# Gate and up of the last six token tiles as one Strassen product, and the convolution moved to the down phase

## What is computed

```python
x = x + 0.5 * ffn(layernorm(x))
x = x + s4(layernorm(x))
x = x + 0.5 * ffn(layernorm(x))

def qlinear(x, q, scale, A, Bm):          # q: int32 levels 0 to 15
    w = (q - 7.5) * (scale * 0.005)[:, None]
    return x @ w.T + 0.02 * (x @ A @ Bm)  # rank 32

ffn(x) = qlinear(silu(qlinear(x, gate...)) * qlinear(x, up...), down...)   # 512 -> 1376 -> 512
s4(u)  = causal convolution of u with a kernel K of length 512, along the features, + D * u
```

## Time and profile before

| | us |
|---|---|
| median of three runs | 608.82 |
| range of the three | 608.34 to 610.92 |
| the profiled execution's own time | 609.25 |
| its span (first to last instruction) | 607.5 |

### The profile page before, as it was taken

How to read it: one execution, slowest core, us unless ns; L and a number is a source line. 1 busy time by engine, 2 the same in 40 slices (tenths; PEclk the granted TensorE clock), 3 DMA queues, 4 the chain that set the end, 5 groups by cost and what they waited for, 6 DMA issues and landing times.

```text
span 607.5 us, 9590 instructions
## 1 busy us (share of the span) xinstructions
PE 584.9 (96%) x3630; PEld 341.3 (56%) x3630; DVE 339.2 (56%) x693; ACT 282.4 (46%) x625; POOL 85.3 (14%) x97
## 2 busy tenths in 40 slices
PE   2799999999999999999999999999999999999997
PEld 2444674457644666445764457644575545754475
DVE  6487575774579727358563584335833467433334
ACT  3676324662277512657226662266623555136631
POOL 4337701100012000023001130012100010000000
PEclk9999999999999999999999999999999999999999
DMA  8994400003002500001301023000322002240001
GB/s 290 397 296 169 70 14 5 1 12 65 13 18 36 81 11 16 18 18 35 75 14 19 17 52 62 10 18 18 68 46 79 1 1 50 29 148 1 0 1 71
DMA packets 67630, 35.63 MB, mean 59 GB/s; under 512 B 56160, under 2 KB 60448, under 8 KB 67584
## 3 DMA queue, kind: packets, MB, share of 16 engines
q1 hardware_dynamic: 66768, 34.87, 22.4%
q10 hardware_dynamic: 816, 0.14, 0.1%
HBM read 17.43 MB, written 4.19 MB: 36 GB/s over the span
## 4 chain that ended last, share of the span: by engine, by line
PE 89%; DVE 5%; ACT 3%; issue 1%; DMA 1%; DVEq 0%; ACTq 0%
PE bank L1062 46%; PE down_acc L1022 27%; PE bank L1078 6%; PE down_acc L1172 4%; PE bank L988 2%; PE bank L1039 2%; PE bank L1155 1%; ACT p_stack L495 1%; DVE z L656 1%; DMA X<-in_x 1%; DVE z L658 1%; DVE zs L649 1%; DVE hT L678 0%; ACT bank L533 0%; ACT PdT L522 0%
## 5 line engine op out<-in xcount | busy, mean ns | idle before, releaser
L1022 PE MATMUL down_acc<-dw,hT 128*128 128x256 f16 (+3 forms) x1408 | 184.4, 286 | 0.0
L533 ACT ACTIVATE bank<-bank,scales 128x512 f32<-128x512 f32 (+1 forms) x176 | 115.8, 659 | 125.7 <-PE bank L1062 125.0
L1062 PE MATMUL bank<-xT,gw 128*128 128x512 f16 (+1 forms) x696 | 164.5, 379 | 2.3 <-ACT work L545 2.1
L1062 PE MATMUL bank<-xT,uw 128*128 128x512 f16 (+1 forms) x696 | 164.5, 379 | 0.2 <-DVE work L722 0.2
L1022 PEld LDWEIGHTS down_acc<-dw,hT 128*128 128x128 f16 (+1 forms) x1408 | 136.0, 98 | 38.5 <-issue 0.6
L722 DVE TENSOR_TENSOR work<-work,bank 128x512 f32<-128x512 f32 (+1 forms) x88 | 60.4, 687 | 138.3 <-PE bank L1078 128.7
L1062 PEld LDWEIGHTS bank<-xT,uw 128*128 128x128 f16 (+1 forms) x696 | 69.6, 100 | 81.1 <-DVE work L722 0.8
L1062 PEld LDWEIGHTS bank<-xT,gw 128*128 128x128 f16 (+1 forms) x696 | 68.4, 100 | 78.7 <-ACT work L545 4.6
L678 DVE SCALAR_TENSOR_TENSOR hT<-work,hT 128x512 f16<-128x512 f32 (+1 forms) x88 | 67.1, 763 | 19.6 <-ACT hT L538 19.5
L538 ACT ACTIVATE hT<-work 128x512 f16<-128x512 f32 (+1 forms) x88 | 55.4, 630 | 31.5 <-DVE work L722 31.5
L545 ACT ACTIVATE work<-bank 128x512 f32<-128x512 f32 (+1 forms) x88 | 51.8, 588 | 10.5 <-PE bank L1078 10.5
(11 more groups left out here) (145 smaller groups left out, 386.5 us busy)
## 6 DMA issues: line engine op xcount, KB each, us to landing
out_x<-X SPq DMA_DIRECT2D x16, 256.0 KB, 2.6
X<-in_x SPq DMA_DIRECT2D x1, 2048.0 KB, 14.8
gq_raw<-in_tables SPq DMA_DIRECT2D x1, 2048.0 KB, 10.5
gq_raw<-in_gate_q_t SPq DMA_DIRECT2D x2, 768.0 KB, 11.6
uq_raw<-in_up_q_t SPq DMA_DIRECT2D x2, 768.0 KB, 11.6
dq_raw<-in_down_q_t SPq DMA_DIRECT2D x1, 1536.0 KB, 14.1
work<-in_b SPq DMA_DIRECT2D x2, 688.0 KB, 9.2
X<-in_x SPq DMA_DIRECT2D x4, 256.0 KB, 5.5
```

The source lines that it names most:

```text
L533: return nc.scalar.activation(acc, acc, ACT.Copy, scale=scales[0:rows[m], g, m:m + 1])
L1022: last = mm(down_acc[b][:, c, 0:width], hT[0:rows[m], m, a, j * P:(j + 1) * P], dw[0:rows[m], m, c, 0:width], start=(m == 0 and a == 0), s ...
L1062: last = mm(dst[0:r, :], w[:, c, cols], xT[:, a, c, :], start=(c == 0 and a == 0), stop=(c == KH - 1 and a == 1))
```

## The change

Tiles 0 and 1 (of eight, counted from 0; `n < FAST`) keep the plain products. In tiles 2 to 7 gate and up of a block are one 2 x 2 product by Strassen's method in Winograd's form. The left factor has the four quarters UP1, UP2, GATE1, GATE2 (up or gate weights, first or second half of K), the right one z's quarters B11, B12, B21, B22 (half of K, half of the 512 tokens). Seven products of 128 rows, K = 256 and 256 tokens (each four matmuls of 256 columns: two chunks, high and low) replace eight.

- The weight sums S1 to S4 are formed once on GpSimd (`weight_sums`, four instructions of 128 x 2752, exact in fp16). z's sums T1 to T4 are formed in f32 on VectorE for each tile (`z_apply`, `z_differences`, `z_sums`), rounded on ScalarE (`z_high`), the rest formed on GpSimd (`z_low`). B12 itself is not kept: `p_product` uses T1 + B11 for it.
- P1, P1+P6 and P1+P6+P7 grow in one bank. ScalarE copies each state, scaled, to SBUF (`t_up`, `t_gate`), and VectorE adds the copies, scaling what stands in the PSUM banks (`up_scaled`, `gate_scaled`), ahead of the low-rank matmuls (now two of 256 columns each for gate and for up).
- h's split into high and low moves from ScalarE and VectorE to GpSimd (`h_split`) in blocks 0 to 9 of the fast tiles.
- The convolution's products and additions move to the down phase of tiles 2 to 5. The state-space part on VectorE moves from tiles 1 and 2 to tile 0's down phase and tile 1, the load of the tables behind the resolvents.
- The down banks are now shared with the blocks' banks; `pd_transpose` and `down_low` share one bank in fast tiles. z's transposes are four per tile, each of 128 tokens x 1792 columns (before: 1024). Many buffers share memory.

The core of the diff:

```diff
-Z_SCALE = 2.0 ** 11
+Z_SCALE = 2.0 ** 9
...
+    FAST = 2
...
+    CONV_IN = 2
...
+    T3, B22, B11, B21, T1, T4, T2 = range(7)
+    UP1, UP2, GATE1, GATE2, S1, S2, S3, S4 = range(0, 16, 2)
...
+            def weight_sums():
+                pool.wait_ge(s_gcast, len(CHUNKS))
+                pool.wait_ge(s_ucast, len(CHUNKS))
+                for i, (o, a, b, op) in enumerate(((S1, GATE1, GATE2, ALU.add), (S3, UP1, GATE1, ALU.subtract),
+                                                   (S2, S1, UP1, ALU.subtract), (S4, UP2, S2, ALU.subtract))):
+                    if i >= 2:
+                        pool.wait_ge(s_wsum, (1, 3)[i - 2])
+                    pool.tensor_tensor(w[:, o:o + 2, :], w[:, a:a + 2, :], w[:, b:b + 2, :], op).then_inc(s_wsum, 1)
...
+            def h_split(n, m):
+                b, r = m % 2, rows[m]
+                pool.wait_ge(f.h[b], uses(n, m) + 1)
+                pool.tensor_scalar(hT[0:r, m, 0, :], h32[0:r, b, :], 1.0, 0.0, ALU.mult, ALU.add)\
+                    .then_inc(f.hhi[b], 1)
+                pool.wait_ge(f.hhi[b], uses(n, m) + 1)
+                pool.tensor_tensor(hT[0:r, m, 1, :], h32[0:r, b, :], hT[0:r, m, 0, :], ALU.subtract)\
+                    .then_inc(f.hlo[b], 1)
...
+            def z_low(n, j, half):
+                q, ops = 2 * (n - FAST) + j, (slice(0, 4), slice(4, 7))[half]
+                pool.wait_ge(f.zq_hi, 4 * q + 3 + half)
+                pool.tensor_tensor(z16[:, j, 1, ops, :], zs[:, ops, :], z16[:, j, 0, ops, :], ALU.subtract)\
+                    .then_inc(f.zq_lo, 1)
...
+            weight_sums()
...
+            for n in range(FAST, N2):
+                more, c = n + 1 < N2, conv_group(n)
+                if c is not None:
                     conv_rstds(c)
-                    conv_low(c * TS)
-                tile_rstds(n + 1, range(0, 2))
-                if convs:
-                    conv_low(c * TS + 1)
-                tile_rstds(n + 1, range(2, TS))
-                if convs:
+                if more:
+                    ln_rstd(n + 1, 0, 1)
+                for m in range(M - 1):
+                    h_split(n, m)
+                    if more and m == 3:
+                        z_low(n + 1, 0, 0)
+                        ln_rstd(n + 1, 2)
+                    if more and m == 4:
+                        z_low(n + 1, 0, 1)
+                    if more and m == 5:
+                        ln_rstd(n + 1, 3)
+                    if c is not None and m in (6, 8):
+                        conv_low(c * TS + (m - 6) // 2)
+                if c is not None:
                     conv_low(c * TS + 2)
...
+            def fast_blocks(n, c):
+                for m in range(M):
+                    s, r, k = m % 2, rows[m], block(n, m)
+                    sums = bank[4 * s + 3][0:r, 0:HH]
+                    act.wait_ge(f.p1, k + 1)
+                    after(act, f.up_s, k - 1)
+                    if m == 1:
+                        act.wait_ge(f.x_out, n * TS)
+                    nc.scalar.activation(t_up[s][0:r, 0, :], sums, ACT.Copy, scale=scales[0:r, 1, m:m + 1])\
+                        .then_inc(f.t11, 1)
+                    act.wait_ge(f.p5, k + 1)
+                    after(act, f.gate_s, k - 1)
+                    nc.scalar.activation(t_gate[s][0:r, 1, :], bank[4 * s + 1][0:r, 0:HH], ACT.Copy,
+                                         scale=scales[0:r, 0, m:m + 1]).then_inc(f.t5, 1)
+                    act.wait_ge(f.p6, k + 1)
+                    nc.scalar.activation(t_up[s][0:r, 1, :], sums, ACT.Copy, scale=scales[0:r, 1, m:m + 1])\
+                        .then_inc(f.t12, 1)
+                    if m:
+                        sum_silu(n, m - 1)
+                    if n + 1 < N2 and 2 <= m <= 5:
+                        z_high(n + 1, 0, m - 2)
+                    if c is not None and m in (1, 7, 9):
+                        conv_norm(c * TS + (1, 7, 9).index(m))
+                    if c is not None and m in (6, 8, 10):
+                        conv_high(c * TS + (m - 6) // 2)
+                    act.wait_ge(f.p7, k + 1)
+                    nc.scalar.activation(t_gate[s][0:r, 0, :], sums, ACT.Copy, scale=scales[0:r, 0, m:m + 1])\
+                        .then_inc(f.t21, 1)
...
+            def z_differences(n, j):
+                q = 2 * (n - FAST) + j
+                dve.wait_ge(f.zs, n * TS + 2 * j + 2)
+                V.tensor_tensor(zs[:, T1:T1 + 2, :], zs[:, 0:2, :], zs[:, B11:B21 + 1, :], ALU.subtract)\
+                    .then_inc(f.z_d, 1)
+                dve.wait_ge(f.z_d, q + 1)
+                V.tensor_tensor(zs[:, T4, :], zs[:, T1, :], zs[:, T4, :], ALU.subtract).then_inc(f.z_t, 1)
+            def z_sums(n, j):
+                q = 2 * (n - FAST) + j
+                dve.wait_ge(f.z_t, 2 * q + 1)
+                V.tensor_tensor(zs[:, T2, :], zs[:, B22, :], zs[:, T1, :], ALU.subtract)
+                V.tensor_tensor(zs[:, T3, :], zs[:, B22, :], zs[:, T3, :], ALU.subtract).then_inc(f.z_t, 1)
...
+            def z_step(n, m):
+                if m == 0:
+                    ln_stats(n, 0, 1)
+                elif m == 4:
+                    ln_stats(n, 2)
+                elif m == 6:
+                    ln_stats(n, 3)
+                elif m in (1, 8):
+                    z_apply(n, m // 8)
+                elif m in (2, 9):
+                    z_differences(n, m // 9)
+                elif m in (3, 10):
+                    z_sums(n, m // 10)
...
+            def up_scaled(n, m):
+                s, r, k = m % 2, rows[m], block(n, m)
+                dve.wait_ge(f.p3, k + 1)
+                dve.wait_ge(f.t12, k + 1)
+                V.scalar_tensor_tensor(up_sums(m), up_sums(m), scales[0:r, 1, m:m + 1], t_up[s][0:r, :, :],
+                                       ALU.mult, ALU.add).then_inc(f.up_s, 1)
+            def gate_scaled(n, m):
+                s, r, k = m % 2, rows[m], block(n, m)
+                dve.wait_ge(f.t21, k + 1)
+                V.scalar_tensor_tensor(gate_sums(m), gate_sums(m), scales[0:r, 0, m:m + 1], t_gate[s][0:r, :, :],
+                                       ALU.mult, ALU.add).then_inc(f.gate_s, 1)
...
+            def fast_blocks(n):
+                for m in range(M + 1):
+                    if m:
+                        up_scaled(n, m - 1)
+                        gate_scaled(n, m - 1)
+                    if n + 1 < N2:
+                        z_step(n + 1, m)
+                    if m:
+                        dve.wait_ge(f.lr_up, block(n, m - 1) + 1)
+                        h_product(n, m - 1, up_sums(m - 1))
...
+                    ops = ((B11, 0), (B21, 2)) if s < 2 else ((T1, 0), (B11, 0), (B22, 2))
+                    terms = [(xT[:, a, 2 * op + k, j * P:(j + 1) * P], c + k)
+                             for op, c in ops for k in range(2) for a in range(2)]
...
+                if n >= FAST:
+                    after(pe, f.dsum, n * TS + j)
...
+            def part(m, dst, blocks, op, first, ks=(0, 1)):
+                r, cols = rows[m], slice(m * P, m * P + rows[m])
+                for k in ks:
+                    for a in range(2):
+                        last = mm(dst[0:r, 0:HH], w[:, blocks + k, cols], xT[:, a, 2 * op + k, :],
+                                  start=(first and k == 0 and a == 0), stop=(k == 1 and a == 1),
+                                  skip_group_check=True)
+                return last
...
+            def fast_blocks(n):
+                c = conv_group(n - 1)
+                for m in range(M):
+                    s, k = m % 2, block(n, m)
+                    up_1, up_2, gate_1, gate_2 = bank[4 * s:4 * s + 4]
+                    if m == 0:
+                        for j in range(2):
+                            pe.wait_ge(f.xTq[j], 32 * (n - FAST + 1))
+                        pe.wait_ge(f.p_stack, (n + 1) * TS)
+                        if n == FAST:
+                            pe.wait_ge(s_wsum, 4)
+                            pe.wait_ge(s_kscale, 1)
+                            pe.wait_ge(f.dsum, n * TS)
+                        if c is not None:
+                            pe.wait_ge(c_out, (c + 1) * TS)
+                    if m == 1:
+                        for b in range(2):
+                            pe.wait_ge(f.d_read[b], 2 * n)
+                    pe.wait_ge(f.silu[s], uses(n, m))
+                    part(m, gate_2, UP1, B11, True).then_inc(f.p1, 1)
+                    part(m, gate_1, GATE2, T4, True)
+                    pe.wait_ge(f.h[s], uses(n, m))
+                    part(m, up_2, S1, T1, True).then_inc(f.p5, 1)
+                    pe.wait_ge(f.t11, k + 1)
+                    part(m, gate_2, S2, T2, False).then_inc(f.p6, 1)
+                    if m == 0:
+                        pe.wait_ge(f.dsum, n * TS)
+                    part(m, up_1, UP2, B21, True, (0,))
+                    if m:
+                        low_rank(n, 0, m - 1)
+                    part(m, up_1, UP2, B21, False, (1,))
```

(69 more changed lines are left out.)

805 lines of the change are left out of this document (436 added, 369 removed).

## The result

The changed kernel takes 611.93 us (median of 20 runs, 610.89 to 617.23), the kernel before 609.42 (20 runs, 608.34 to 610.92). The ratio of the means is 1.0067 [1.0044, 1.0091]: 0.7% slower (0.4% by the medians), where the forecast was 600.0 with a range of 588 to 614. The profiled execution took 616.48 us (span 614.4); it is one of nine of the 20 that stand at 616.5 to 617.2, the other eleven stand at 610.9 to 612.0.

A forecast was written before the change was run, and what follows sets the result against it. The prediction took TensorE's nearly gapless stream of columns as the bound. Its terms, -25.1 + 2.7 + 2.1 + 1.2 + 2.4 + 4.0 + 4.0 = -8.7 us, took the profiled 609.25 to 600.5, adjusted to the median 600; range 588 to 614.

The forecast's parts named there:

- Weight sums: Tile 0's down phase: VectorE's last h split and an X addition wait for GpSimd's sums, +4 us, bounds 0 and 10.
- Gate and up: Blocks of six tiles: fewer matmul columns on TensorE, a tile's 42.7 us become 38.5, -25.1 us in all.
- Start of a tile: Block 1 of tiles 3 and 4: low-rank product waits 1.2 us for VectorE's scaled sums, +2.4 us.
- End of a tile: Before the last down transpose: TensorE waits about 0.35 us for ScalarE's P split and PdT copy, six times, +2.1 us.
- Tile 2's start: Tile 2's first product waits for tile 1's last dsum behind the Toeplitz split on VectorE, +1.2 us, between 0 and 3.5.
- The lock within a block: Fast blocks: z's differences at block 9 wait for GpSimd, 0.8 us late, five tiles, +4.0 us, bounds 0 and 15.
- ScalarE's copies: Within a fast block: 256-column copies out of PSUM taken at 0.40 us each, between 0.15 and 0.66, and covered.
- +2.7: Low-rank P: two of four P products have 12 matmuls in place of 8, 0.45 us a tile, six times.
- (3): Rival: GpSimd paces the fast blocks, five tiles each lose about 3.5 us, 618 us; chance 0.20.
- (2): Rival: VectorE or ScalarE paces the blocks, 3.85 us instead of 3.50, 606 to 612 us; chance 0.15.

The follow-up runs named there:

- e1: Changed kernel without the four weight sums, original weight blocks in place of S1 to S4 (wrong results in tiles 2 to 7): 600.11 us.
- e7: Changed kernel with the third weight sum also waiting for the second, so two stand back to back: 612.14 us.
- e2: Changed kernel with each weight sum on GpSimd waiting for the one before: 608.28 us.
- e3: Changed kernel with the weight sums on VectorE, two behind the last h split of tile 0 and two behind that of tile 1: 599.50 us.
- e9: As e3, fast tiles' h split back on ScalarE and VectorE, the high half behind the same block's last copy: 613.78 us.
- e5: As e3, fast tiles' h split back on ScalarE and VectorE, the high half behind the next block's silu: 676.45 us.
- e4: Changed kernel with the sums on GpSimd cut into 32 pieces of 344 columns, each waiting for the one before: 603.53 us.
- e6: As e8, and tile 0's first reciprocals moved behind P's split in its down phase: 593.70 us.
- e8: As e3, in fast tiles one of two statistics moved from block 0 to 1 and first-half z steps one block later: 595.14 us.

## Why the prediction was wrong

The failed step is **"Weight sums"**, "+4, bounds 0 and 10". The instruction was sized well (forecast 5.9 us, measured 5.46), and the forecast named two kinds of victim, the last h split and the X additions. It failed in assuming that each "can wait for the rest of a 5.9 us instruction". The split of block 9, which it didn't count, waited for three sums, since they stood back to back (TensorE waited 9.23 us for it), and the last one for the fourth (5.07): 14.3 us of waiting for h, where it had "some 2 us". The low clock adds more, as the P products above show. In tile 0's down phase the sums cost 16.6 us (44.6 against e1's 28.0), and 11.8 by the medians of the whole: above the bound of 10 either way. The X additions weren't hit at all, as the stall had carried them past the sums' end.

The Trainium skill (SBUF — State Buffer, Who interferes with whom) says that a VectorE instruction with two SBUF inputs contends with a GpSimd one that reads SBUF, calls the shared port pair an exclusive lock, and has issue order decide who blocks. The rows agree on which instructions are hit (17.00 us for L893, 0.68 for L887). By that rule alone the wait is one instruction's length, which is what I took; the 17.00, 11.67 and 6.33 us of the changed kernel, e7 and e2 show that a waiting VectorE isn't let in between two that stand back to back. Nor did the order of issue help: in the changed kernel the split stands at 69.80 and the first sum at 70.19.

The rest of the sum, step by step:

- **Gate and up**, -25.1 (3.50 us a block): right. The low-rank products of tile 2 come at 199.03 and 202.52, 3.49 apart, in slots of 0.109 (two start-to-start slots of low-rank products are 0.22):

```profile
199.03 0.38 PE L1315 MATMUL banks<-PT,gb_w 128*128 128x256 f16 x2 [0.17 <-DVE banks L908]
...
202.52 0.38 PE L1315 MATMUL banks<-PT,gb_w 128*128 128x256 f16 x2
```

- **Start of a tile**, stall 1.2 in tiles 3 and 4: right in place and cause. Tile 3's stands at 1.64 us, the sum is 4.1 in five waits, against +2.4. The forecast put the low-rank product 50 slots into the tile, but block 0 has no low-rank products, so it is 46, or 5.0 us; with that its own sum gives 6.7 - 5.0 = 1.7:

```profile
272.16 0.38 PE L1315 MATMUL banks<-PT,gb_w 128*128 128x256 f16 x2 [1.64 <-DVE banks L908]
```

- **End of a tile**, 0.35 us each: wrong, it costs nothing. The wait is there with 0.22 us, but the kernel before has one of the same length in each tile, ahead of its third `down_low`, and there it is gone: 1.6 us in seven waits in both profiles. The first row is of the kernel before, the second of the changed one:

```profile
306.78 0.39 PE L1039 MATMUL bank<-db_w,PdT 128*128 128x512 f16 x1 [0.22 <-ACT PdT L522]
...
338.23 0.39 PE L1292 MATMUL banks<-db_w,PdT 128*128 128x512 f16 x1 [0.22 <-ACT PdT L622]
```

- **Tile 2's start**: 1.3 against +1.2. TensorE's wait for the Toeplitz matrix's maximum grew from 0.3 to 1.1 us, which the sum doesn't have.
- **The lock within a block**, +4.0: too dear. The differences of z did take 1.26 us, as forecast, and ahead of them the two scalings of z, which I hadn't named, took 2.29 in place of 0.99. But only one low-rank product between them is late: one block of 3.82 us and the next of 3.56 in each of tiles 2 to 5, 0.4 a tile, some 1.5 in all:

```profile
223.02 2.29 DVE L833 TENSOR_SCALAR zs<-X,meanvar,rstd 128x512 f32<-128x512 f32 x2
...
227.16 1.26 DVE L840 TENSOR_TENSOR zs<-zs 128x512 f32<-128x512 f32 x1
```

- **ScalarE's copies** of 256 columns took 0.474 us against 0.40, and stayed covered.
- **Not in the sum**: the state-space vectors (2.0 us) and reciprocals (1.73) ahead of P's split in tile 0's down phase. The prediction costed no move of them; it took 1.75 us. Nor does it have the 2.0 us ahead of the down phase.

From tile 1's start on, the terms -25.1 + 2.7 + 2.1 + 1.2 + 2.4 + 4.0 = -12.7 stand against the measured -13.6. That they come so close is partly luck: +2.1 that didn't come and +4.0 that was 1.5 stand against starts too small by 1.7. With the sizes found, and 66 blocks shorter by 3.88 - 3.495, it is -25.4 + 2.7 + 0 + 1.3 + 0.8 + 4.1 + 1.5 = -15.0, and the 1.4 between them stays open. Tiles 3 and 4 each take 73.13 us in place of 74.61 where the terms give -1.4. In e3, without the sums on GpSimd, the whole kernel takes 599.5. The forecast without its +4 is 596, so its 600 and this 599.5 agree by luck too; but most of the gain that I saw in the change is there once four instructions stand elsewhere. Of the rivals, GpSimd didn't pace the fast blocks (3), nor VectorE or ScalarE (2), but only since the h split had moved: e9, where it is back, is at rival 2's block length and 613.8 us, in the one order that I tried besides e5's. The forecast's own ending on the slow side put GpSimd in tiles 3 to 7, and not in tile 0, where the few instructions were that decided.

## What to carry to other kernels

Long instructions on GpSimd with no wait between them act, for VectorE's SBUF-to-SBUF instructions, as one long one. Before such work is put "in the free time" of GpSimd, list the VectorE instructions with two SBUF inputs that fall into its stretch and who waits for them, and put it on VectorE if that has a gap: here 1.6 us in place of 5.46, and 12 us for the kernel. Splitting it is no cure where a chain of many small VectorE instructions runs beside it, and pulling one victim out of the stretch may push the next into it.

## What the runs showed of the hardware that I had not expected

- Two-input VectorE instructions stay locked out through GpSimd instructions that stand back to back (17.00, 11.67, 6.33 us for three, two, one of 5.46), and get in where GpSimd waits for a semaphore, even one that its own last instruction raises.
- In e4 also the two-column TENSOR_SCALAR with its scalar and its input in SBUF took 0.88 us beside the pieces, and 0.22 in e3, and a two-column copy from SBUF 0.42 against 0.15. VectorE's large instructions with an input in PSUM kept their times (0.69 and 0.68 us).
- After the wait of 9.23 us TensorE ran at 0.50 of full speed up to 96 us. A wait of 2.03 us at 29 us was followed by a stretch at 0.57 in the changed kernel's profile (the eight matmuls behind it took 3.39 us) and by full speed in that of e3 (1.90), with the same instructions ahead of it. All four profiled executions of the changed kernel have the low stretch, and those of e2, e6, e7 and e8; those of before, e1, e3, e4, e5 and e9 don't. What decides it stays open.
- A two-input fp16 instruction of 2752 columns took 1.6 us on VectorE (3.40 once, beside GpSimd) and 5.46 on GpSimd.
